# A feed-forward kernel on one core: the first batch's attention in two halves, and layer 1 of the first 512 tokens in two passes

## The chip, the cores and the metric

The kernel runs on one core of a Trainium2 chip. A core has TensorE (matrix products into PSUM, eight banks of 128 x 512 fp32), VectorE (DVE), ScalarE (ACT), GpSimd (POOL) and SyncE (SP), which here only issues DMAs. Each engine works through its own list of instructions in order, and semaphores tie the lists together. The metric is the device time of one execution in microseconds (us).

## What is computed

Eight sequences of 256 tokens with 256 features pass a cross-attention-like block and a feed-forward network of four layers, each with a layer norm in front and a residual behind. Cut to what matters:

```python
def xattn(x, c):                                # x: 8 x 256 x 256, c = ctx: 8 x 120 x 256
    s = einsum('eth,efh->etf', x, c)            # "score"
    h = gelu_tanh(s) * s                        # "gate"
    return einsum('etf,efh->eth', h, c)         # "weigh"

x = x + xattn(layernorm(x), ctx)
t = layernorm(x)
h = silu(t @ w1.T * w1_s) * (t @ w2.T * w2_s)   # layer 1: 256 -> 1024, twice
h = gelu(h @ h1.T * h1_s)                       # 1024 -> 1024
h = gelu(h @ h2.T * h2_s)                       # 1024 -> 1024
x = x + h @ w3.T * w3_s                         # 1024 -> 256
```

## The kernel before

A batch `b` is one sequence, 256 tokens, kept as two halves `j` of 128 tokens (`xs[:, 2b+j, :]`). Two batches make a tile `t` of 512 tokens, which is what the feed-forward layers work on.

**The attention of a batch** is a chain over all engines. DVE takes the statistics of both halves (`stats` = `spread`, two BATCH_NORM_STATS2, and `gather`, two aggregates). POOL makes the reciprocal deviation (`rstd`, two instructions). DVE normalizes (`scale`, one instruction per half). TensorE transposes (`turn(0,b)`). ScalarE copies the result to SBUF (`copy_t`). TensorE multiplies by the context (`score`), ScalarE applies gelu (`act_s`), DVE multiplies (`gate`), TensorE multiplies by the context again (`weigh`), DVE adds the residual (`add_in`). Then comes the second norm in the same way (`stats(1,b)`, `rstd`, `scale(1,b)`, `turn(1,b)`). Its result is split for the fp32r products: ScalarE copies it rounded into `X[..,0,..]` (`first`), and DVE writes what rounding left out into `X[..,1,..]` (`second`, semaphore `s_X1`). Every intermediate of a batch lies in one PSUM bank, `side(b)` = `P[6 + b % 2]`.

**Layer 1 of a tile** is 16 groups `i` of four products (two halves of the contraction, rounded part and rest): `i = 2m` is column block `m` of `w1`, `i = 2m+1` that of `w2`. Six PSUM banks take turns by the table `TURN`. Behind a pair of groups ScalarE does `silu(t,m)` into one of two buffers `SL`, and DVE does `both(t,m)`, which multiplies the second product by it. A group that reuses a bank waits for the `silu` or the `both` that read it (`first_free`, `consumed`). In `layer1(0)` of ScalarE, `hi8` rounds a finished block for the next layer, and DVE's `lo8` takes the rest.

**The order of TensorE around the change** is written out by hand: spins (products whose results nobody reads, `SPIN`), the attention of batches 0 and 1 woven together, then the first six groups of tile 0 for batch 0's 256 columns alone, with `turn(1,1)` behind the fourth. When `s_X1` says that batch 1's columns are there, the same six groups follow for them, and `layer1(0)` does the other ten groups over all 512 columns. `attend` puts `turn(0,2)` and `turn(0,3)` behind group 10. Then `eight(0)` starts on the next layer: eight products, `score(2)` and `score(3)`, and so on. Each of the products `i` of `eight` needs 1 MB of weights, which SP loads back from a DRAM copy into the ring `WR` (`load_w8`), behind other loads in the one queue. The weights of layer 1 are loaded into `stage` and rounded by ScalarE into `W12` (`copy_w(0)` to `copy_w(3)`, semaphore `s_cp`; a group of `w1` needs three of them, one of `w2` all four).

ScalarE needs its Silu table before `silu(0,0)`; the call `table(ACT.Silu)` on a spare tile makes the load stand ahead of it.

## Time and profile before

| | us |
|---|---|
| median of 3 runs | 340.02 |
| lowest and highest | 339.81, 340.51 |
| the profiled execution | 339.02 |
| its span in the profile | 337.1 |

The profile shows one execution. Its busy shares say little here, since TensorE is busy in nearly all of the span; what matters is where TensorE is not, and for whom it waits there. The views to read are the chain of work that ended last, in order of time, and the timelines of the single engines in the first 60 us. In the timelines a row merges instructions of one kind that follow each other; the time in brackets is how long the engine was idle before it, and who ended that. TensorE was granted its full clock in every slice of the page.

### The profile page before, as it was taken

To read this page: it belongs to the slowest core of one execution; us is meant where nothing else is said; L and a number is where in the kernel's file an instruction comes from. 1 tells how busy PE (TensorE), PEld (TensorE's weight loads), DVE (VectorE), ACT (ScalarE), POOL (GpSimd) and SP (SyncE) were. 2 spreads that over 40 slices of the span, in tenths; PEclk is the share of its full clock that TensorE was granted. 3 is DMA by queue.
4 is the path that set the end of the run, shared out by engine and by line. 5 is a ranking of instruction groups with operands and counts; after the bars stand their busy time and mean duration, and the time that the engine had idled before them with its cause. 6 is when DMAs were issued, how large, how long until landed. Compare 5 with 4: busy or idle time off the path is not lost.

```text
span 337.1 us, 4680 instructions
## 1 busy us (share of the span) xinstructions
PE 327.9 (97%) x1628; PEld 276.9 (82%) x1628; DVE 254.0 (75%) x465; ACT 205.0 (61%) x327; POOL 17.9 (5%) x40
## 2 busy tenths in 40 slices
PE   6699999999999999999999999999999999999996
PEld 4588888888888888888899888888888888888895
DVE  4576879639968697897777534697978698977885
ACT  2655625384844464867794244469587769557960
POOL 3130023002202000000000000000000000000000
PEclk9999999999999999999999999999999999999999
DMA  7799999699939769334540550026655636333003
GB/s 231 258 372 408 398 392 405 227 349 383 319 136 325 266 189 328 140 130 144 192 161 0 162 213 0 1 92 243 228 189 187 207 122 234 124 124 126 1 0 134
DMA packets 22541, 68.61 MB, mean 204 GB/s; under 512 B 1632, under 2 KB 3040, under 8 KB 18784
## 3 DMA queue, kind: packets, MB, share of 16 engines
q1 hardware_dynamic: 22512, 68.25, 56.8%
q8 instruction: 15, 0.25, 0.3%
q14 instruction: 14, 0.11, 0.1%
HBM read 57.75 MB, written 18.87 MB: 227 GB/s over the span
## 4 chain that ended last, share of the span: by engine, by line
PE 95%; DVE 2%; DMA 1%; ACT 0%; issue 0%; POOL 0%; SPq 0%; DVEq 0%
PE P L1176 45%; PE P L1240 17%; PE P L1129 17%; PE P L1266 9%; PE P L1077 2%; PE P L1093 2%; PE P L1085 2%; DMA xs<-in_x 1%; DVE st L753 1%; DVE xs L782 0%; DVE X L789 0%; DVE xn L766 0%; SPq L358 0%; POOL rs L472 0%; ACT X L545 0%
## 5 line engine op out<-in xcount | busy, mean ns | idle before, releaser
L1176 PE MATMUL P<-TR,WR 128*128 128x512 f32 x672 | 152.6, 389 | 0.0
L1176 PEld LDWEIGHTS P<-TR,WR 128*128 128x128 f32 x672 | 126.1, 188 | 26.2
L831 DVE TENSOR_TENSOR TR<-H,TR 128x512 fp32r<-128x512 f32 x84 | 57.5, 688 | 19.0 <-ACT TR L569 16.9
L569 ACT ACTIVATE TR<-H 128x512 fp32r<-128x512 f32 x84 | 52.5, 629 | 21.4 <-DVE H L826 16.2
L1129 PE MATMUL P<-X,W 128*128 128x512 f32 (+1 forms) x280 | 60.4, 373 | 2.0 <-DVE X L789 2.0
L1240 PE MATMUL P<-TR,WR 128*128 128x512 f32 x256 | 61.3, 395 | 0.0
L1129 PEld LDWEIGHTS P<-X,W 128*128 128x128 f32 x280 | 49.1, 188 | 11.2 <-DVE X L789 2.4
L1240 PEld LDWEIGHTS P<-TR,WR 128*128 128x128 f32 x256 | 47.8, 188 | 9.7
L804 DVE SCALAR_TENSOR_TENSOR H<-P,sc,SL 128x512 f32<-128x512 f32 x32 | 23.9, 746 | 23.4 <-PE P L1129 18.2
L559 ACT ACTIVATE SL<-P,sc 128x512 f32<-128x512 f32 x32 | 22.1, 690 | 31.7 <-PE P L1129 31.4
L610 ACT ACTIVATE H<-H,sc 128x512 f32<-128x512 f32 x36 | 25.9, 720 | 15.5 <-DVE H L847 15.4
L1266 PE MATMUL P<-WR,TR 128*128 128x256 f32 x256 | 31.3, 283 | 0.0
L826 DVE TENSOR_TENSOR H<-H 128x512 f32<-128x512 f32 x48 | 31.2, 685 | 0.0
L1266 PEld LDWEIGHTS P<-WR,TR 128*128 128x128 f32 x256 | 31.0, 192 | 0.2
L853 DVE SCALAR_TENSOR_TENSOR SL<-SL 128x1024 f32<-128x1024 f32 x22 | 26.8, 1218 | 1.4 <-ACT SL L503 1.4
L847 DVE TENSOR_TENSOR H<-P,H 128x512 f32<-128x512 f32 x36 | 24.4, 684 | 4.0 <-PE P L1176 4.0
L837 DVE TENSOR_TENSOR TR<-H,TR 128x512 fp32r<-128x512 f32 x32 | 20.9, 688 | 6.6 <-ACT TR L590 6.4
L598 ACT ACTIVATE H<-P 128x512 f32<-128x512 f32 x36 | 21.5, 597 | 6.2 <-PE P L1176 3.8
L590 ACT ACTIVATE TR<-H 128x512 fp32r<-128x512 f32 x32 | 19.2, 627 | 2.3 <-PE P L1266 2.3
L503 ACT ACTIVATE SL<-WR 128x1024 f32<-128x1024 f32 x14 | 14.8, 1055 | 9.0 <-DVE SL L853 9.0
L584 ACT ACTIVATE H<-P,sc 128x512 f32<-128x512 f32 x16 | 9.7, 689 | 12.2 <-PE P L1240 12.2
L753 DVE BATCH_NORM_STATS2 st<-xs 128x6 f32<-128x256 f32 x32 | 12.0, 416 | 4.3 <-DMA xs<-in_x 4.0
(50 smaller groups left out, 203.9 us busy)
## 6 DMA issues: line engine op xcount, KB each, us to landing
WR<-blocks_h SPq DMA_DIRECT2D x27, 1024.0 KB, 4.8
H<-in_h SPq DMA_DIRECT2D x8, 1024.0 KB, 12.0
blocks_h<-H SPq DMA_DIRECT2D x8, 1024.0 KB, 6.3
blocks_h<-in_h SPq DMA_DIRECT2D x7, 1024.0 KB, 14.0
stage<-in_w SPq DMA_DIRECT2D x4, 512.0 KB, 7.2
WR<-last_w SPq DMA_DIRECT2D x2, 1024.0 KB, 4.9
xs<-in_x SPq DMA_DIRECT2D x7, 256.0 KB, 11.1
out<-xs SPq DMA_DIRECT2D x6, 256.0 KB, 6.4
```

Of the source, the lines that this page charges most:

```text
L559: eng.activation(SL[:, g % 2, :], P[TURN[t][i % 6]][:, :], ACT.Silu, scale=sc[:, m:m + 1]).then_inc(s_sl, 1)
L569: eng.activation(TR[:, f % RING, 0, :], operand(c, L, s, kk), ACT.Copy).then_inc(s_hi, 1)
L610: eng.activation(to, src, ACT.Gelu, scale=sc[:, col:col + 1]).then_inc(s_ge, 1)
L804: eng.scalar_tensor_tensor(out=source(t // 2, 0)[:, m, t % 2, :], in0=P[TURN[t][i % 6]][:, :], scalar=sc[:, 8 + m:9 + m], in1=SL[:, g % 2, :],
L826: eng.tensor_tensor(tile(src, to, kk), tile(src, one, kk), tile(src, two, kk), ALU.subtract).then_inc(s_td, 1)
L831: eng.tensor_tensor(TR[:, f % RING, 1, :], operand(c, L, s, kk), TR[:, f % RING, 0, :].bitcast(f32), ALU.subtract).then_inc(s_lo, 1)
L847: eng.tensor_tensor(to, bank(c, L, s, m)[:, :], other, ALU.add).then_inc(s_cd, 1)
L853: eng.scalar_tensor_tensor(out=a, in0=a, scalar=1.0, in1=a, op0=ALU.is_ge, op1=ALU.not_equal, accum_out=fl[:, i:i + 1]).then_inc(s_fl, 1)
L1129: out_ = eng.matmul(P[TURN[t][i % 6]][:, lo_:hi_], w, X[:, t % 2, h, k, lo_:hi_], start=(k == 0 and h == 0), stop=(k == 1 and h == 1))
L1176: out_ = eng.matmul(bank(c, L, s, m)[:, :], WR[r % WRING][:, at:at + 128], TR[:, f % RING, h, :], start=(s in FRESH and kk == 0 and h == 0 ...
L1240: out_ = eng.matmul(bank8(i, m)[:, :], WR[r % WRING][:, at:at + 128], TR[:, f % RING, h, :], start=(i % 2 == 0 and kk == 0 and h == 0), st ...
L1266: out_ = eng.matmul(P[n][:, at], TR[:, f % RING, h, j * 128:(j + 1) * 128], WR[r % WRING][:, k * D:(k + 1) * D], start=(k == 0 and h == 0 ...
```

## The change

The attention of batch 0 is done in two halves of 128 tokens, each with its own PSUM bank (`piece(0)` = `P[6]`, `piece(1)` = `P[5]`) and its own semaphores for the first half (`e_...`). For it there are new functions on every engine, one per step, with the same operations on half the elements. Layer 1 of tile 0 becomes two passes of 16 groups over 256 columns, `p = 0` for batch 0 and `p = 1` for batch 1. Both passes have their own `silu` and `both` over 256 columns. `weigh(1)`, `turn(1,1)` and `turn(0,2)` of TensorE are moved into pass one (behind groups 3, 12 and 14), `score(2)` goes between the passes, and `turn(0,3)` stays behind group 10 of pass two. Pass one uses the banks in the order `TURN0`. The spins go to `P[0]`, and the first lot has 16 instead of 20. SP's list of DMAs is unchanged.

On VectorE the first pass stood like this before (from the second norm of batch 1 on):

```order
L766 TENSOR_SCALAR xn<-xs,mv,rs 128x256 x2
L753 BN_STATS st<-xs 128x6 x2
L757 BN_AGGR mv<-st 128x2 x2
L789 TENSOR_TENSOR X<-P,X 128x2x256
L753 BN_STATS st<-xs 128x6 x2
L757 BN_AGGR mv<-st 128x2 x2
L804 SCALAR_TENSOR_TENSOR H<-P,sc,SL 128x512 x2
L766 TENSOR_SCALAR xn<-xs,mv,rs 128x256 x2
L804 SCALAR_TENSOR_TENSOR H<-P,sc,SL 128x512
```

Here L766 is `scale`, L753 and L757 are `stats`, L789 is `second`, L804 is `both`. In the changed kernel (L897 is `both`, L875 `add_in`, L812 and L816 `stats`, L825 `scale`, L882 `second`):

```order
L897 SCALAR_TENSOR_TENSOR H<-P,sc,SL 128x256 x2
L875 TENSOR_TENSOR xs<-P,xs 128x512
L812 BN_STATS st<-xs 128x6 x2
L816 BN_AGGR mv<-st 128x2 x2
L897 SCALAR_TENSOR_TENSOR H<-P,sc,SL 128x256 x2
L812 BN_STATS st<-xs 128x6 x2
L816 BN_AGGR mv<-st 128x2 x2
L897 SCALAR_TENSOR_TENSOR H<-P,sc,SL 128x256
L825 TENSOR_SCALAR xn<-xs,mv,rs 128x256 x2
L897 SCALAR_TENSOR_TENSOR H<-P,sc,SL 128x256
L825 TENSOR_SCALAR xn<-xs,mv,rs 128x256 x2
L897 SCALAR_TENSOR_TENSOR H<-P,sc,SL 128x256 x2
```

Batch 1's residual, its second norm and the statistics of batch 2 have moved from ahead of the first `both` to between the `both` of pass one; right behind these rows stands `second(1)`.

On TensorE pass one ends, and pass two begins, like this in the changed kernel (L1238 is a group, four rows' worth of 128x256 each; L1186 a turn; L1194 `score(2)`; L1348 the first products of `eight(0)`):

```order
L1238 MATMUL P<-X,W 128x256 x8
L1186 MATMUL P<-ident,xn 128x128 x4
L1238 MATMUL P<-X,W 128x256 x4
L1194 MATMUL P<-xt,cf 120x256 x2
L1238 MATMUL P<-X,W 128x256 x44
L1186 MATMUL P<-ident,xn 128x128 x4
L1238 MATMUL P<-X,W 128x256 x20
L1348 MATMUL P<-TR,WR 128x512 x8
L1194 MATMUL P<-xt,cf 120x256 x2
```

Before, 20 wide products stood in front of `eight(0)`, and both scores behind its first eight:

```order
L1129 MATMUL P<-X,W 128x512 x20
L1240 MATMUL P<-TR,WR 128x512 x8
L1085 MATMUL P<-xt,cf 120x256 x4
L1240 MATMUL P<-TR,WR 128x512 x32
L1093 MATMUL P<-ct,hh 128x256 x4
```

On ScalarE the last steps ahead of the first Silu are in another order. Before (L525 is `copy_w`, L545 `first`, L521 the table, L559 `silu`, L577 `hi8`):

```order
L525 ACTIVATE W<-stage 128x1024 x2
L545 ACTIVATE X<-P 128x2x256
L525 ACTIVATE W<-stage 128x1024
L545 ACTIVATE X<-P 128x2x256
L521 ACT_TABLE_LOAD
L521 ACTIVATE spare<-mhalf 128x2
L559 ACTIVATE SL<-P,sc 128x512 x2
```

After (L564 is `copy_w`, L599 the halves of `first`, L570 `copy_t(1)`, L577 `act_s(1)`, L613 `silu`):

```order
L564 ACTIVATE W<-stage 128x1024 x2
L599 ACTIVATE X<-P 128x2x128
L570 ACTIVATE xt<-P 128x512
L564 ACTIVATE W<-stage 128x1024
L599 ACTIVATE X<-P 128x2x128
L564 ACTIVATE W<-stage 128x1024
L577 ACTIVATE gl<-P 120x256
L560 ACT_TABLE_LOAD
L560 ACTIVATE spare<-mhalf 128x2
L613 ACTIVATE SL<-P,sc 128x256 x7
```

`copy_t(1)` and `act_s(1)` of the second batch have moved behind the first batch's halves, and `act_s(1)` now stands right ahead of the table load.

The diff, cut to its core (the halves on DVE, ScalarE and POOL are the old steps over half the elements):

```diff
-SPIN = (20, 3, 3, 4, 4)
+TURN0 = (2, 3, 4, 5, 0, 1)
+SPIN = (16, 3, 3, 4, 4)
...
+        def piece(j):
+            return P[(6, 5)[j]]
...
+        def tokens1(t, p):
+            return slice(p * TB, (p + 1) * TB) if t == 0 else slice(0, TT)
...
@@ ScalarE
             def layer1(t):
+                for m in range(8 if t == 0 else 0):
+                    silu(0, m, 0)
+                    if m == 6:
+                        first(1)
+                    if m == 7:
+                        copy_t(2)
                 for m in range(8):
                     silu(t, m)
                     if t == 0 and m == 6:
-                        copy_t(2)
                         copy_t(3)
...
-            copy_t(0)
-            act_s(0)
+            copy_half(0)
+            act_half(0)
+            copy_half(1)
+            act_half(1)
+            copy_w(0)
+            copy_w(1)
+            first_half(0)
             copy_t(1)
-            copy_w(0)
+            copy_w(2)
+            first_half(1)
+            copy_w(3)
             act_s(1)
-            copy_w(1)
-            copy_w(2)
-            first(0)
-            copy_w(3)
-            first(1)
             table(ACT.Silu)
...
@@ VectorE
             def layer1(t):
+                for m in range(8 if t == 0 else 0):
+                    both(0, m, 0)
+                    if m == 1:
+                        add_in(1)
+                        stats(1, 1)
+                    if m == 3:
+                        stats(0, 2)
+                    if m == 4:
+                        scale(1, 1)
+                    if m == 5:
+                        scale(0, 2)
+                    if m == 7:
+                        second(1)
+                        stats(0, 3)
                 for m in range(8):
                     both(t, m)
-                    if t == 0 and m in (1, 2):
-                        scale(0, m + 1)
+                    if t == 0 and m == 2:
+                        scale(0, 3)
...
+            stats_half(0, 0)
+            stats_half(0, 1)
+            scale_half(0, 0)
+            spread(0, 1)
+            scale_half(0, 1)
+            gather(0, 1)
+            gate_half(0)
+            add_half(0)
+            stats_half(1, 0)
+            gate_half(1)
             scale(0, 1)
+            add_half(1)
+            scale_half(1, 0)
+            stats_half(1, 1)
+            second_half(0)
+            scale_half(1, 1)
+            second_half(1)
             gate(1)
...
@@ TensorE
             def layer1(t):
-                if t:
-                    eng.wait_ge(s_X1, 2 * t + 2)
+                if t == 0:
+                    eng.wait_ge(s_X1, 1)
+                    for i in range(16):
+                        if i < 2:
+                            eng.wait_ge(s_cp, 3 + i)
+                        if i >= 6:
+                            consumed(0, i - 6, 0)
+                        group(0, i, 0).then_inc(s_mm1, 1)
+                        if i == 3:
+                            weigh(1)
+                        if i == 12:
+                            turn(1, 1)
+                        if i == 14:
+                            turn(0, 2)
+                    score(2)
+                eng.wait_ge(s_X1, 2 * t + 2)
                 for i in range(16):
-                    if t == 0 and i < 6:
-                        continue
                     first_free(t, i)
                     group(t, i).then_inc(s_mm1, 1)
                     attend(t, i)
...
             spin(SPIN[0])
-            turn(0, 0)
+            turn_half(0, 0)
             spin(SPIN[1])
-            score(0)
+            score_half(0)
+            turn_half(0, 1)
             spin(SPIN[2])
+            weigh_half(0)
+            score_half(1)
+            spin(SPIN[3])
+            weigh_half(1)
             turn(0, 1)
-            weigh(0)
+            turn_half(1, 0)
+            spin(SPIN[4])
+            turn_half(1, 1)
             score(1)
-            spin(SPIN[3])
-            weigh(1)
-            spin(SPIN[4])
-            turn(1, 0)
-            eng.wait_ge(s_X1, 1)
-            for i in range(6):
-                if i < 2:
-                    eng.wait_ge(s_cp, 3 + i)
-                group(0, i, 0, TB)
-                if i == 3:
-                    turn(1, 1)
-            eng.wait_ge(s_X1, 2)
-            for i in range(6):
-                group(0, i, TB, TT).then_inc(s_mm1, 1)
             layer1(0)
```

## Rows read from the trace of the kernel before

**Rows 1.** The page: DMA share in 40 slices; the chain by engine.
```profile
DMA  7799999699939769334540550026655636333003
...
PE 95%; DVE 2%; DMA 1%; ACT 0%; issue 0%; POOL 0%; SPq 0%; DVEq 0%
```

**Rows 2.** The chain in order of time: start us, length us, what.
```profile
1.63 3.44 DMA xs<-in_x
...
17.01 2.18 PE P L1129 x16
...
20.30 0.70 DVE X L789
...
21.04 7.71 PE P L1129 x44
28.75 0.87 PE P L1077 x8
29.62 4.55 PE P L1129 x20
34.17 1.81 PE P L1240 x8
35.99 1.73 PE P L1085 x8
...
62.15 0.87 PE P L1077 x8
...
172.46 15.35 PE P L1266 x128
```

**Rows 3.** Timeline of TensorE: start us, length us, what, count.
```profile
34.01 1.98 PE L1240 MATMUL P<-TR,WR 128*128 128x512 f32 x8
```

**Rows 4.** Timeline of VectorE, first 26 us.
```profile
3.06 0.79 DVE L753 BATCH_NORM_STATS2 st<-xs 128x6 f32<-128x256 f32 x2 [3.06 <-DMA xs<-in_x]
...
9.57 0.42 DVE L773 TENSOR_TENSOR hh<-P,gl 120x256 f32<-120x256 f32 x1 [1.41 <-ACT gl L538]
11.28 0.69 DVE L782 TENSOR_TENSOR xs<-P,xs 128x512 f32<-128x512 f32 x1 [1.28 <-PE P L1093]
12.01 0.75 DVE L753 BATCH_NORM_STATS2 st<-xs 128x6 f32<-128x256 f32 x2
...
12.96 0.39 DVE L773 TENSOR_TENSOR hh<-P,gl 120x256 f32<-120x256 f32 x1
...
24.89 0.75 DVE L804 SCALAR_TENSOR_TENSOR H<-P,sc,SL 128x512 f32<-128x512 f32 x1
25.55 0.73 DVE L766 TENSOR_SCALAR xn<-xs,mv,rs 128x256 f32<-128x256 f32 x2
```

**Rows 5.** Timeline of ScalarE, first 23 us.
```profile
9.15 0.39 ACT L538 ACTIVATE gl<-P 120x256 f32<-120x256 f32 x1 [1.28 <-PE P L1085]
...
16.01 1.05 ACT L525 ACTIVATE W<-stage 128x1024 fp32r<-128x1024 f32 x1
19.66 0.60 ACT L545 ACTIVATE X<-P 128x512 fp32r<-128x512 f32 x1 [2.61 <-PE P L1077]
20.28 1.28 ACT L521 ACT_TABLE_LOAD   x1
21.58 0.20 ACT L521 ACTIVATE spare<-mhalf 128x2 f32<-128x2 f32 x1
21.89 0.69 ACT L559 ACTIVATE SL<-P,sc 128x512 f32<-128x512 f32 x1
```

**Rows 6.** Timeline of GpSimd, one `rstd` of a batch.
```profile
13.13 0.22 POOL L470 TENSOR_SCALAR rs<-mv 128x2 f32<-128x2 f32 x1 [5.81 <-DVE mv L757]
13.43 0.71 POOL L472 TENSOR_TENSOR rs<-rs,mhalf 128x2 f32<-128x2 f32 x1
```

**Rows 7.** Timeline of SyncE's queue; the 12.95 issue waited for `stage[3]` to land.
```profile
12.95 0.61 SPq L295 DMA_DIRECT2D blocks_h<-in_h  x1
...
44.19 0.42 SPq L308 DMA_DIRECT2D WR<-blocks_h  x1
```

**Rows 8.** DMA issues of 44.15 to 44.45 us, with median us to landing.
```profile
WR<-blocks_h SPq DMA_DIRECT2D x1, 1024.0 KB, 14.4
```

## What the change does to the time: the prediction

> **What bounds the kernel now.** I read the page's chain first: 95% of what ended last is TensorE's work [rows 1], so nothing else can matter for long. The chain in order of time then says where the rest is [rows 2]: up to 17.01 us it hops between all engines through the first batch's attention. From 17.01 TensorE works, loses about half a us before 21.04 (it waits for the second batch's `X`, which DVE starts at 20.30), and from 21.04 on its pieces follow each other without a hole to the end. So only two things can move the time: when the last product of layer 1 of the first 512 tokens is out of TensorE, and how much TensorE work there is. The mark that I compare is the start of the first eight products of `eight(0)`: 34.01 us before [rows 3]. Since the change does `score(2)` ahead of that mark and before did it behind, where two scores took 1.73 us [rows 2], the mark of before that is like for like is 34.01 + 0.87 = 34.88 us.
>
> **TensorE's own cost of two passes.** A product over 256 columns takes 0.120 us (128 in 15.35 us), one over 512 takes 4.55/20 = 0.228 us [rows 2]. Before, 48 narrow and 40 wide ones: 14.9 us. After, 128 narrow ones: 15.4 us. So 0.5 us more work, all of it on the path. A turn is 0.44 us, a score or weigh 0.87 us [rows 2]; these are moved, their number stays. Pass one is 64 x 0.120 + `weigh(1)` 0.87 + two turns 0.87 = 9.4 us; pass two is 7.7 + one turn 0.44 = 8.1 us. The four spins fewer in the first lot are work that nobody waits for: the first transposes wait for the statistics, not for TensorE.
>
> **The prologue in halves.** Sizes I don't have are taken between rows. DVE: 256 elements 0.42 us, 512 0.69 [rows 4]; 128 elements I put at 0.29. ScalarE: 256 at 0.39, a copy of 512 at 0.60 [rows 5], 128 at 0.28. POOL needs 0.31 + 0.71 us for an rstd, plus about 0.1 of hop on either side [rows 6]. Hops between other engines are 0.02 to 0.15 us. The first batch is there when DVE starts at 3.06 [rows 4], the second at 5.07 [rows 2].
> Half 0: statistics to 3.65, rstd to 4.74, scale to 5.25, transposes to 5.75, copy 6.15, score 6.95 (context landed before), gelu 7.25, gate 7.57, weigh 8.38, add 8.82, statistics 9.45, rstd 10.55.
> Half 1 follows through the same engines: its weigh ends at 10.50, its add at 10.94. Then `scale_half(1,0)` to 11.38, statistics of half 1 to 11.89, rstd to 12.99, `scale_half(1,1)` to 13.50, transposes to 14.00, `first_half(1)` to 14.40, `second_half(1)` to 14.85. Group 0 of pass one may start at 14.90, and the next at about 15.45, because ScalarE does `copy_w(3)` (1.05 us [rows 5]) only after `first_half(1)`; its data are there at 12.95 [rows 7]. As group 0 takes 0.48, I count pass one from 14.95 us: 2.06 us earlier than the first products before.
> If that were all, pass two would end at 14.95 + 9.4 + 8.1 = 32.5 and the gain would be 2.4 us. Two new waits eat it.
>
> **New wait one: who feeds pass one.** Behind `first_half(1)` (14.40) ScalarE has `copy_w(3)` to 15.35, `act_s(1)` to 15.64, and then the table load: from 20.28 to the first Silu at 21.89 is 1.61 us [rows 5], so the first Silu starts at 17.27. It lasts 0.48 over 256 columns (0.69 for 512 [rows 5], less 0.21 as between gelu and copy there), so DVE's first product of the pass (`both`) starts at 17.76. A `both` over 256 columns I cost at 0.40 us from start to start: 0.65 for 512 (24.89 to 25.55) less some 0.25 by which 256 elements are cheaper (0.69 to 0.42) [rows 4]. In front of `scale(1,1)` stand five of them, `add_in(1)` (0.72, 11.28 to 12.01) and two rounds of statistics (0.95 each, 12.01 to 12.96 [rows 4]): 2.00 + 0.72 + 1.90 = 4.62. So `scale(1,1)` starts at 22.38 and its second half is out at 23.1. TensorE comes to `turn(1,1)`, which waits for it, at 14.95 + 13 x 0.48 + 0.87 = 22.06 and leaves it at about 23.37 instead of 22.5: 0.9 us lost. Nothing of before shows this wait; there the same turn stood after four groups and only the second batch's own half hung on it. Queued behind it are three groups and `turn(0,2)`: pass one ends at 23.37 + 3 x 0.48 + 0.44 = 25.25.
>
> **New wait two: the hand-over between the passes.** `second(1)` stands behind the last `both` of pass one on DVE. The last product is visible about 0.2 us after TensorE could go on, `both` takes 0.40 to the next start, `second(1)` 0.67, hops 0.08: 1.35 us, of which `score(2)` fills 0.87 without shortening it. Pass two starts at 26.60 and ends at 26.60 + 8.1 = 34.7 us. Within pass two DVE needs for two groups of a column block 0.40 and ScalarE about the same, plus half of a 512-wide split (some 0.3 each): 0.7 against TensorE's 0.96, so no further wait.
>
> **The sum.** 34.7 against 34.88: 0.2 us gained. Behind the mark the order of the work is the same on all engines, and TensorE has no hole there, so the 0.2 us goes to the end. The profiled execution took 339.02 us (span 337.1 and 1.9 around it), it becomes 338.8; the median of the three runs lies 1.0 above it, and I take the difference over to it: 340.02 - 0.2 = 339.8 us.
>
> **A cap further on.** The weights of the fourth product of `eight(0)` are asked for at 44.19 [rows 7] and land 14.4 us later [rows 8], at 58.6. The DMA engines are busy without a break then (the 9s of the page's DMA line from its seventh slice of 8.4 us back to its fourth [rows 1]), so asking earlier doesn't bring them sooner. TensorE comes to them at 62.15 - 1.8 = 60.3 of the chain [rows 2], 60.1 in start times. So no more than about 1.5 us of any gain ahead of them can reach the end: even a perfect pass one stops at 338.5 us. With 0.2 us gained it costs nothing.
>
> **A rule that speaks against the change.** The load of the Silu table lasts 1.28 us, and the small ACTIVATE behind it starts 0.02 us after its end [rows 5]. "ScalarE: Activation LUTs" of the Trainium skill, in What ACT_TABLE_LOAD costs, puts a drain of about 1.38 us beside each load of 1.28 us. This case's rows show no such drain on either side of the load.
>
> **The rivals.**
> A, my forecast: both new waits, 339.8 us; unsure by 0.6 us either way from the prices of the 128-wide steps (each by 0.05, some ten in a row) and of `both`.
> B, DVE is early enough at `turn(1,1)`: should the first Silu start 0.9 us sooner, or the statistics run shorter, only the hand-over is left. Then pass two starts at 14.95 + 9.4 + 1.35 = 25.7 and the mark is at 33.8: 1.1 us gained, 338.9 us. For it: DVE is idle from the end of its prologue to 17.76. Against: the rows of the table load are fixed and ScalarE has `copy_w(3)` and `act_s(1)` in front of it.
> C, the other side: the 256-wide steps of pass one cost nearly as much as 512-wide ones, start to start 0.65 instead of 0.40. Place: the five `both` before `scale(1,1)`, then the last one before `second(1)`. 6 x 0.25 = 1.5 us later, the mark at 36.2: 1.3 us slower, 341.3 us. It is slower than before by what can be measured from a price of 0.55 on. For it: no row of before has this instruction at 256. Against: a TENSOR_TENSOR out of PSUM has 0.42 at 256 [rows 4].
> D, no new wait at all and the cap decides: 338.5 us. It needs `second(1)` ahead of the last `both`, which the order denies.
> E, a drain of 1.4 us in front of or behind the table load that has merely not been visible: both new waits move by it, 34.7 + 1.4 = 36.1, 341.2 us. The rows leave it a chance of 1 in 100. (By the page named above this is what would come.)
>
> **Chances.** A 0.62, B 0.17, C 0.12, D 0.03, E 0.01, something not seen 0.05. What a measurement of this kernel can tell from no change is about 0.2%, or 0.7 us. A reaches beyond that on the fast side in about one case in six, on the slow side in one in fifteen. Faster 0.12 + 0.15 + 0.03 = 0.30; slower 0.04 + 0.12 + 0.01 + 0.02 = 0.19; same 0.51. The range takes in B and most of the way to C: 338.7 to 340.9 us.
>
> **What would show it.** First product of layer 1 at 14.9 (right if 14.6 to 15.4); first Silu at 17.3; a hole or late turn of TensorE of 0.9 us at `turn(1,1)` around 22 to 23.4, released by DVE's `xn`; a second start of layer 1 at 26.6, released by DVE's `X`; `both` over 256 columns at 0.48 us each; `eight(0)` at 34.7; no wait for weights near 60. I am wrong if `both` is above 0.6, if the first Silu is not near 17.3, or if TensorE has holes behind 35 us.

## The result, and the profile after it

| | before, beside it | changed |
|---|---|---|
| median | 339.28 us (22 runs) | 340.43 us (22 runs) |
| lowest and highest | 338.74, 341.57 | 339.99, 341.78 |
| the profiled execution, its span | 339.02, 337.1 | 340.34, 338.6 |

The changed kernel is slower: ratio 1.003, 95% interval 1.0019 to 1.0042. That is 1.0 us, or 1.15 between the medians, where 0.2 us of gain was forecast. In the profiled executions it is 1.3 us, and 1.4 of span (338.56 less 337.13 in the trace's hundredths). 340.43 lies inside the range by luck: of the kernel before, 15 of the 22 executions lie between 338.7 and 339.5 us and seven between 339.8 and 341.6, for a reason that no trace shows, and the three whose median of 340.02 was my base are all among the seven. Counted from 339.28, the forecast would have been 339.1 us and the range 338.0 to 340.2, and 340.43 is outside it.

First the place that I argued about. The timeline of TensorE in the changed kernel, start us, length us, what, and in brackets the idle time ahead and who ended it:

```profile
15.14 2.18 PE L1238 MATMUL P<-X,W 128*128 128x256 f32 x16
17.16 1.03 PE L1202 MATMUL P<-ct,hh 120*128 120x256 f32 x4
17.84 4.67 PE L1238 MATMUL P<-X,W 128*128 128x256 f32 x36
22.87 0.76 PE L1186 MATMUL P<-ident,xn 128*128 128x128 f32 x4 [0.36 <-DVE xn L825]
...
25.80 1.09 PE L1194 MATMUL P<-xt,cf 128*120 128x256 f32 x4 [0.30 <-ACT xt L570]
26.67 5.54 PE L1238 MATMUL P<-X,W 128*128 128x256 f32 x44
...
34.87 2.00 PE L1348 MATMUL P<-TR,WR 128*128 128x512 f32 x8
```

The first products of layer 1 start at 15.14 us instead of 17.01 [rows 2], TensorE then waits at `turn(1,1)` and at the hand-over, and `eight(0)` starts at 34.87 against the like-for-like mark of 34.88. The attention in halves and the passes have cancelled almost exactly.

The piece near 62 us and the last add of VectorE say that nothing happens behind it either. The chain in order of time has

```profile
62.22 0.87 PE P L1186 x8
```

where the kernel before has it at 62.15 [rows 2], and the timeline of VectorE at the end reads, first in the changed kernel, then in the one before:

```profile
334.63 0.42 DVE L1055 TENSOR_TENSOR xs<-Y,xs 128x256 f32<-128x256 f32 x1
```
```profile
334.56 0.42 DVE L962 TENSOR_TENSOR xs<-Y,xs 128x256 f32<-128x256 f32 x1
```

0.07 us later, and yet the span ends 1.4 us later. The rest is behind the last piece of work. VectorE's last step is a branch over the fallback (`with eng.If(v != 0)`, which recomputes everything if a test of the rounding fails and is never entered), and then the DRAIN at the kernel's end. By line (operation, count, durations in ns, first and last start in us), in the changed kernel:

```profile
L1145 DVEq COMPARE_BRANCH  x1: 76/76/76, 335.2 to 335.2; - x1
...
L54 DVEq DRAIN  x1: 61/61/61, 338.3 to 338.3; - x1
...
L54 SPq DRAIN  x1: 7/7/7, 337.2 to 337.2; - x1
```

and in the kernel before:

```profile
L1036 DVEq COMPARE_BRANCH  x1: 76/76/76, 335.1 to 335.1; - x1
...
L52 DVEq DRAIN  x1: 59/59/59, 335.7 to 335.7; - x1
...
L52 SPq DRAIN  x1: 7/7/7, 336.9 to 336.9; - x1
```

The views round to tenths; in the trace's hundredths the exit, from the start of the branch to the start of the DRAIN, took 0.57 us before and takes 3.05 us now. Before, SyncE, which waits until the last output has landed, was the last (336.90); now VectorE is, at 338.27. Not all of the difference is VectorE's: SyncE's own end moved to 337.24, since the last output, issued 0.07 us later, took 1.98 us to land for 1.72. So about 0.3 of the 1.4 us is that landing, and 1.0 us (338.27 less 337.24) is what the exit adds. Neither the page's chain nor a view of waits by work shows this, since no engine is busy; the 95% that the chain gave to TensorE [rows 1] was true, and the difference lies in the part that it leaves out.

### The profile page after: what moved, and what is told of

The parts are those of the page before. It is cut to its first block, busy times and chain, and to the rows that moved or that the text cites. A ratio compares the mean times of both kernels' runs of the same rounds, so it can differ in the third digit from the quotient of the medians.

```text
span 338.6 us, 4807 instructions
## 1 busy us (share of the span) xinstructions
PE 329.3 (97%) x1668; PEld 278.9 (82%) x1668; DVE 256.3 (76%) x476; ACT 207.2 (61%) x338; POOL 19.4 (6%) x44
## 4 chain that ended last, share of the span: by engine, by line
PE 96%; DVE 2%; issue 1%; POOL 0%; ACT 0%; POOLq 0%; DVEq 0%
PE P L1285 45%; PE P L1348 17%; PE P L1238 17%; PE P L1374 9%; PE P L1202 2%; PE P L1186 2%; PE P L1194 2%; PE P L1384 1%; PE P L1437 0%; PE P L1423 0%; DVE xs L851 0%; DVE xn L839 0%; DVE st L832 0%; PE P L1430 0%; ACT xt L570 0%
## 5 line engine op out<-in xcount | busy, mean ns | idle before, releaser
L924 DVE TENSOR_TENSOR TR<-H,TR 128x512 fp32r<-128x512 f32 x84 | 57.5, 689 | 18.5 <-ACT TR L623 16.4
L1238 PE MATMUL P<-X,W 128*128 128x512 f32 (+1 forms) x320 | 61.4, 349 | 0.1
L1348 PE MATMUL P<-TR,WR 128*128 128x512 f32 x256 | 61.4, 395 | 0.0
L1238 PEld LDWEIGHTS P<-X,W 128*128 128x128 f32 x320 | 51.7, 189 | 8.1 <-DVE X L857 0.5
L1348 PEld LDWEIGHTS P<-TR,WR 128*128 128x128 f32 x256 | 47.7, 188 | 9.7
L613 ACT ACTIVATE SL<-P,sc 128x512 f32<-128x512 f32 (+1 forms) x40 | 24.0, 604 | 34.1 <-PE P L1238 33.4
L897 DVE SCALAR_TENSOR_TENSOR H<-P,sc,SL 128x512 f32<-128x512 f32 (+1 forms) x40 | 25.4, 640 | 23.9 <-PE P L1238 16.0
L498 POOL TENSOR_TENSOR rs<-rs,mhalf 128x2 f32<-128x2 f32 x14 | 11.0, 785 | 1.2
```

The lines of the kernel that those rows point to most:

```text
L613: eng.activation(SL[:, g % 2, at], bank1(t, 2 * m, p)[:, at], ACT.Silu, scale=sc[:, m:m + 1]).then_inc(s_sl, 1)
L897: eng.scalar_tensor_tensor(out=source(t // 2, 0)[:, m, t % 2, at], in0=bank1(t, 2 * m + 1, p)[:, at], scalar=sc[:, 8 + m:9 + m], in1=SL[:, ...
L924: eng.tensor_tensor(TR[:, f % RING, 1, :], operand(c, L, s, kk), TR[:, f % RING, 0, :].bitcast(f32), ALU.subtract).then_inc(s_lo, 1)
L1238: out_ = eng.matmul(bank1(t, i, p)[:, at], w, X[:, t % 2, h, k, at], start=(k == 0 and h == 0), stop=(k == 1 and h == 1))
L1348: out_ = eng.matmul(bank8(i, m)[:, :], WR[r % WRING][:, at:at + 128], TR[:, f % RING, h, :], start=(i % 2 == 0 and kk == 0 and h == 0), st ...
```

## The experiments

**The fallback shorter.** In the changed kernel the fallback's loops ran over 7 batches instead of 8 on every engine, so the branch skips 194, 27 fewer.

```diff
-                for b in range(NB):
+                for b in range(NB - 1):
```

> The changed kernel, with the fallback at the end (the branch that is never taken in these runs) written for 7 batches instead of 8 on every engine; the eighth batch of the fallback is left out, nothing of what is executed is. On VectorE the jump over the fallback gets 25 instructions shorter. Theory 1 (the lost time is VectorE's jump over the fallback: 3.0 us from the branch to the next instruction in the changed kernel, 0.5 us before, because the place it jumps to has to be fetched): VectorE leaves its last block near 335.8 instead of 338.3, span 337.1 to 337.3, time 1.3 us less than the changed kernel, so 0.0 to 0.1% above the kernel before. Theory 2 (the end takes longer because the kernel has 11 semaphores more or because the 256-column passes cost later): nothing changes, ratio to before 1.003, span 338.6.

Measured: 339.14 us, ratio 0.9982 [0.9961, 1.0004]. The exit is short again, from 335.4 us to

```profile
L54 DVEq DRAIN  x1: 59/59/59, 336.0 to 336.0; - x1
```

So the whole loss goes away with code that is never run. Its semaphores and its order of work are the changed kernel's: that rival falls.

**The kernel before, 11 instructions longer.** Eleven one-column memsets on VectorE while it waits for the first data:

```diff
+            for i in range(11):
+                eng.memset(padt[:, i:i + 1], 0.0)
```

> The kernel before, with 11 writes of one column of a spare tile at the start of VectorE's list, where it has 3 us of idle time, so that VectorE executes as many instructions ahead of its last branch as in the changed kernel. Theory 1 (the place of VectorE's branch in its list of instructions decides whether the place it jumps to is at hand): VectorE leaves its last block 2.5 us later, span 338.5, time 1.3 to 1.5 us above before (ratio 1.004), with TensorE's last product where it was. Theory 2 (semaphores, or the attention halves themselves): no change, ratio 1.000.

Measured: 340.32 us, ratio 1.0028 [1.001, 1.0046], and the same long exit:

```profile
L1039 DVEq COMPARE_BRANCH  x1: 76/76/76, 335.3 to 335.3; - x1
...
L52 DVEq DRAIN  x1: 64/64/64, 338.2 to 338.2; - x1
```

Eleven tiny instructions at the start of the kernel before cost as much as the whole change. This is the cleanest evidence, since nothing of the change is in it. The number 11 was meant to bring the branch to the changed kernel's place, which is really 21 further on; that 11 is slow as well was luck.

**The changed kernel with 117 and with 107 instructions more.** With 107, 27 stand at the start and 5 behind each of 16 late `both` (shown here); with 117, 5 at the start and 7 behind each. With 107 the list is 128 longer than before, with 117 it is 138.

```diff
+            for i in range(27):
+                eng.memset(padt[:, i:i + 1], 0.0)
...
+                    for i in range(5 if t >= 2 else 0):
+                        n = 27 + 40 * (t - 2) + 5 * m + i
+                        eng.memset(padt[:, n:n + 1], 0.0)
```

> The changed kernel with 117 writes of one column of a spare tile on VectorE, 5 at its start and 7 behind each of the 16 last multiplications of layer 1, where it waits for TensorE. Before the change VectorE ran 11 instructions less, so its branch now stands 128 instructions behind the place it had before the change; the instruction fetches in the trace are 8192 bytes, which would be 128 instructions of 64 bytes. Theory 1 (the place within such a block decides): VectorE's jump is short again, 0.5 us, span 337.1 to 337.4 and ratio 1.000 to 1.001, although the list is longer than ever. Theory 1b (more instructions make it longer whatever their place): the jump stays at 3 us, ratio 1.003. Theory 2: as 1b, span 338.6.

> The changed kernel with 107 writes of one column of a spare tile on VectorE (27 at its start, 5 behind each of the 16 last multiplications of layer 1). Counted in the traces, waits that are instructions of their own included, VectorE's list has 631 records in the changed kernel and 610 before the change, 21 more and not 11; with 117 more it stood 10 past a full block of 128, where the jump was still long, as with 11 more ahead of the kernel before. With 107 it stands exactly 128 behind the kernel before. Theory 1 (place within a block of 8192 bytes): the time from VectorE's branch to its next instruction falls from 3.0 to 0.5 us, span 337.2, ratio to before 1.000 plus what the 107 writes cost VectorE, at most 0.3 us. Theory 1b (the longer the list, the worse): 3.0 us, ratio 1.003.

Measured: 117 gives 340.45 us, ratio 1.003 [1.0015, 1.0044], exit 3.04 us. The number 117 came from the page's count of VectorE's busy instructions, which grew by 11 (465 to 476); the list itself grew by 21, so this run stands at 138, ten past a full 128, and is long like the kernel before with its 11 more. 107 gives 339.12 us, ratio 0.9999 [0.9984, 1.0015], exit 0.58 us:

```profile
L1151 DVEq COMPARE_BRANCH  x1: 76/76/76, 334.9 to 334.9; - x1
...
L54 DVEq DRAIN  x1: 60/60/60, 335.5 to 335.5; - x1
```

The kernel of the change, complete, with 107 useless instructions more, is as fast as the one before. "The longer the slower" falls, and a period of 128 fits.

**Which places are slow.** The kernel before with 64 and with 107 memsets more, one execution each:

> The kernel before with VectorE's list 64 one-column memsets longer (32 at its start, 2 behind each of 16 late `both`), so about 674 records instead of 610. The jump over the fallback skips some 220 instructions. Theory (it is slow when two borders of a block of 128 instructions lie between the branch and its target, quick when only one does; the borders follow from the runs so far: the target of the kernel before is less than 11 instructions ahead of one): 64 further on the branch is still in the same block and the target in the one behind the next, so the exit takes 3 us and the span grows by 1.2 to 1.5 us. Rival (only a target in the first few dozen places behind a border is slow): the target is some 55 places behind the border, the exit takes 0.6 us, the span 337.1 to 337.4.

> The kernel before with VectorE's list 107 one-column memsets longer (27 at its start, 5 behind each of 16 late `both`), so about 717 records. Theory (number of borders between branch and target): 107 further on the branch has passed the next border itself, only one lies between it and the target again, the exit takes 0.6 us and the span stays at 337.1 to 337.4. Rival (short only where the target stands at the end of a block, as in the kernel before and 128 later): the target is 96 to 107 places behind the border, not at the end, the exit takes 3 us, the span 338.4 to 338.8.

Measured: 64 gives 340.41 us, span 338.6; 107 gives 338.97 us, span 337.2; the kernel before ran 339.46 beside them. The exits, of 64 first, then of 107:

```profile
L52 DVEq DRAIN  x1: 61/61/61, 338.3 to 338.3; - x1
```
```profile
L52 DVEq DRAIN  x1: 59/59/59, 335.8 to 335.8; - x1
```

The traces so far together, with the place counted from the kernel before:

| kernel | branch, places on | skipped | exit us | span us |
|---|---|---|---|---|
| before | 0 | 221 | 0.57 | 337.1 |
| before, 11 more | 11 | 221 | 2.87 | 338.4 |
| changed | 21 | 221 | 3.05 | 338.6 |
| before, 64 more | 64 | 221 | 3.06 | 338.6 |
| before, 107 more | 107 | 221 | 0.58 | 337.2 |
| changed, 107 more | 128 | 221 | 0.58 | 337.2 |
| changed, 117 more | 138 | 221 | 3.04 | 338.9 |
| changed, short fallback | 21 | 194 | 0.57 | 337.4 |

The span of the row of 64 says little: its last output took 2.75 us to land (1.70 to 2.04 in the other traces), so that SyncE ended at 338.14 us and the exit added only 0.2 us. What it shows is the exit of 3.06 us.

One rule holds for all eight rows, and for the six traces of the experiments further down (places 5, 16 and three times 21 with 194 skipped, and 128 with 221, all short): with borders every 128 instructions, the exit is short where one border lies between branch and target, long where two do. The target of the kernel before lies less than 11 places ahead of a border; 11, 21 and 64 further on it is behind it, at 107 the branch itself has crossed the border below, and with 27 instructions fewer to skip the target falls back ahead of it. The exits of 64 and 107 came out as written down beforehand. The rows don't prove the counting of borders, though: that an exit is long wherever the target stands in the first 60 or so places of a block, and short from about 100 on, fits them too, wherever the branch is. What they do show is that the target's place matters (with 221 and 194 skipped the branch is at the same place 21), and that both 0 and 128 are short while 11 and 138 are long. The mechanism behind it, that the target's block must first be fetched, the traces bear out only in part: instruction packets of one queue average 8 KB,

```profile
q14 instruction: 14, 0.11, 0.1%
```

and from VectorE's branch to the end of the trace there are two such packets in each of the four traces with a long exit, and one in each of the ten others. But which packet VectorE waited for I could not tell. In "Runtime: NRT & Kernel Launch" of the Trainium skill, under Instruction fetch mechanics, it says that a taken branch with a target outside the current two pages of instructions has to wait for a fetch. The direction agrees with the 3.05 us. The size of 256 instructions that the same section gives for a page of instructions doesn't: a jump over 221 would then never leave two neighbouring ones, and the rows fit a period of 128.

**The halves alone.** The first batch's attention in halves, but layer 1 as before (six groups over 256 columns, then wide ones), with `weigh(1)` behind the fourth group and `turn(1,1)` behind the sixth; the fallback short, as in all that follow but the last.

```diff
-            turn(0, 0)
+            turn_half(0, 0)
...
             eng.wait_ge(s_X1, 1)
             for i in range(6):
...
                 group(0, i, 0, TB)
```

> The kernel before with the first part of the change alone (attention of batch 0 in halves, the order of that part as in the changed kernel), layer 1 of the first 512 tokens as before, turn(1,1) behind the first six half groups; fallback for 7 batches. Theory A (the halves make batch 0 early at batch 1's cost, which only two passes can use): the first product of layer 1 at 15.1, TensorE then idle from about 19 until batch 1's columns are there at 22.7, eight(0) at 35.5 instead of 34.0, ratio 1.0045. Rival (the halves are a gain of their own): eight(0) at or before 34.0.

Measured: 344.01 us (4 runs), ratio 1.0167 [1.0108, 1.0225]. TensorE:

```profile
14.92 2.18 PE L1213 MATMUL P<-X,W 128*128 128x256 f32 x16
...
21.46 0.88 PE L1161 MATMUL P<-ident,xn 128*128 128x128 f32 x4 [2.53 <-DVE xn L808]
23.75 9.93 PE L1213 MATMUL P<-X,W 128*128 128x256 f32 x44 [1.41 <-DVE X L865]
...
38.94 1.98 PE L1324 MATMUL P<-TR,WR 128*128 128x512 f32 x8
```

The page's clock line, and ScalarE's first Silu:

```profile
PEclk9978999999999999999999999999999999999999
```
```profile
25.08 0.69 ACT L600 ACTIVATE SL<-P,sc 128x512 f32<-128x512 f32 x1 [0.59 <-PE P L1213]
```

The direction was right, the size far off: 38.94 us where I had written 35.5. The second start of layer 1 is at 23.75 us where I had written 22.7, and the 44 products behind it take 9.93 us for 7.71 [rows 2]. The latter is TensorE's clock: it was idle from 18.9 to 21.46 us and again, but for four transposes, to 23.75, and from 22.0 to 28.6 us the granted clock was 0.50, the lower of its two levels (1.2 GHz), and full again from 28.8 us on, after TensorE had worked without a hole since 23.75. Before 28.8 us a product over 256 columns takes 0.21 us from start to start for 0.12; from there on a product over 512 takes 0.23, as before. No bank is missing: TensorE waits for nothing after 23.75, and the first Silu waits 0.59 us for TensorE. In the changed kernel the clock stays full. Without the passes the early first products are of no use: TensorE runs out of work for batch 0, waits for batch 1, and loses 2.2 us more to the clock.

**The passes alone.** The attention whole, layer 1 in two passes; `turn(1,1)` behind group 3, `second(1)` behind the second `both`.

```diff
+                for m in range(8 if t == 0 else 0):
+                    both(0, m, 0)
+                    if m == 1:
+                        second(1)
```

> The two passes alone: the first batch's attention stays whole as before (first products of layer 1 near 17.0 us), layer 1 of the first 512 tokens in two passes of 256; `turn(1,1)` stays behind group 3 and `second(1)` stands behind the second `both` of pass one, so that nothing hangs on the hand-over. The fallback that the branch jumps over is cut to 7 batches, so that VectorE's exit is short. Theory (the halves bring the first product 2 us forward, the two waits and the half us of narrow products eat it; each part has its own share): first Silu 18.7 instead of 21.9, pass one 17.0 + 64 x 0.120 + two turns 0.87 = 25.6 us, no hole between the passes, pass two 8.1 and `score(2)` 0.87: `eight(0)` at 34.6 us, 0.3 us ahead of the like-for-like 34.88 of before; ratio 0.999. Rival (two passes cost more than the count of products says, because ScalarE or VectorE can't keep up with 256-wide groups while they also do `first(1)` and `second(1)`): holes of TensorE within pass one, `eight(0)` behind 35.5, ratio 1.002 or more.

Measured: 339.33 us, ratio 1.0014 [0.9997, 1.0031]: not to be told from before.

```profile
16.89 2.17 PE L1223 MATMUL P<-X,W 128*128 128x256 f32 x16 [1.54 <-DVE X L876]
...
25.99 1.09 PE L1179 MATMUL P<-xt,cf 128*120 128x256 f32 x4 [0.30 <-ACT xt L565]
...
35.03 2.00 PE L1333 MATMUL P<-TR,WR 128*128 128x512 f32 x8
```

35.03 us against 34.6 expected: pass one runs without a hole, though in 8.8 us for the 8.55 counted, and `score(2)` then waits 0.30 us for ScalarE's copy of the third batch, a wait I hadn't reckoned with here. No engine failed to keep up, so the rival for this run falls. With the halves the mark was 34.87: coming 1.75 us earlier at the start (15.14 against 16.89), they have brought 0.16 us at the mark.

**Feeding pass one better.** If the two waits eat the gain, taking away what makes them should return it. First the statistics of the third batch ahead of the first `both`, and the scales earlier (GpSimd's order to match):

```diff
             gate(1)
+            stats(0, 2)
...
-                    if m == 3:
-                        stats(0, 2)
-                    if m == 4:
-                        scale(1, 1)
-                    if m == 5:
-                        scale(0, 2)
+                    if m == 2:
+                        scale(0, 2)
+                    if m == 3:
+                        scale(1, 1)
```

> The changed kernel with the fallback for 7 batches (its eighth batch left out, nothing that is executed), and on VectorE the statistics of batch 2 moved from behind the fourth multiplication of pass one to the idle time ahead of the first, scale(0,2) behind the third and scale(1,1) behind the fourth; GpSimd takes batch 2's deviation ahead of batch 1's second. Theory A (VectorE's lateness at turn(1,1) costs TensorE what the prediction said): turn(1,1) leaves TensorE 0.7 us sooner, pass two starts at 25.9 instead of 26.7, eight(0) at 34.1 instead of 34.9, and as VectorE's jump is short too, 0.7 us below the kernel before, ratio 0.998. Rival (pass one is bound by TensorE and the hand-over alone, or gives the time back at the weights near 60 us): eight(0) at 34.7 to 34.9 or a wait for weights behind it, ratio 1.000.

Then, besides, `second(1)` ahead of the last `both`, and `score(2)` behind group 2 of pass two:

```diff
-                    if m == 7:
+                    if m == 6:
                         second(1)
+                    if m == 7:
                         stats(0, 3)
...
-                    score(2)
                 eng.wait_ge(s_X1, 2 * t + 2)
...
+                if (t, i) == (0, 2):
+                    score(2)
```

> As the kernel with batch 2's statistics moved, and the hand-over between the passes taken away: second(1) stands ahead of the last multiplication of pass one, and score(2) behind the third group of pass two instead of between the passes. Theory A: TensorE goes from pass one into pass two without a hole, pass two starts at 24.8, eight(0) at 33.8, ratio 0.997; the wait for the weights of the fourth product of eight(0) (59 to 60 us) is still not reached. Rival (the DMA cap is nearer than 1.5 us): TensorE waits there and the ratio stays at 0.998 or above.

Measured: the first 338.70 us, ratio 0.9989 [0.9972, 1.0006], `eight(0)` at 34.22 us; the second 338.29 us, ratio 0.9964 [0.9947, 0.998], `eight(0)` at 33.68. Both marks came within 0.12 us of what was expected. In the second, pass two follows pass one without a hole:

```profile
22.21 0.67 PE L1186 MATMUL P<-ident,xn 128*128 128x128 f32 x4
...
24.04 2.29 PE L1238 MATMUL P<-X,W 128*128 128x256 f32 x16
26.16 1.03 PE L1194 MATMUL P<-xt,cf 128*120 128x256 f32 x4
26.83 4.18 PE L1238 MATMUL P<-X,W 128*128 128x256 f32 x32
...
33.68 2.00 PE L1348 MATMUL P<-TR,WR 128*128 128x512 f32 x8
```

So the two waits cost 1.2 us at the mark (34.87 less 33.68) of the 1.87 us by which the first products come earlier. The rest is work that the change puts between the first products and the mark: `weigh(1)`, 0.87 us, stood ahead of them before, and the narrow products take 0.5 us more; against that, the wait of 0.47 us ahead of 21.04 is gone. This adds up to within about 0.2 us. And the cap further on shows, although I had expected that it would still not be reached. The chain of the second version, in order of time:

```profile
45.37 14.64 DMA WR<-blocks_h
60.01 0.04 issue
60.05 2.11 PE P L1348 x8
```

TensorE waits 0.8 us there for the weights of the fourth product, and the profiled execution, the slowest of its ten, gives the gain back (339.07 us); the median doesn't.

**The loads of batches 6 and 7 behind those weights.** 0.5 MB ahead of them less, once with the short fallback, once with the whole one and the 107 memsets:

```diff
-            load_x(6)
-            load_x(7)
             load_raw(3)
             sums_out(0)
             load_w8(3)
+            load_x(6)
+            load_x(7)
```

> The version with the feeding of pass one reordered (statistics of the third batch ahead of the first `both`, `second(1)` ahead of the last one, `score(2)` in pass two; fallback of 7 batches) and, besides, the loads of batches 6 and 7 (0.5 MB) put behind the load of the fourth product's weights in SyncE's list. Theory (the cap: those weights land at a time set by how many bytes stand ahead of them, at 370 to 400 GB/s, not by when they are asked for): they land 0.5 MB / 0.39 = 1.3 us earlier, near 58.6 us instead of 60.0; the wait of 0.8 us for `WR` near 60 is gone, the last add of VectorE comes 0.8 us earlier than without the move, ratio 0.9945 to 0.996. Rival (the wait is set by the round trip of the stored block or by the queue's order of service): landing stays near 60, the wait of 0.3 to 0.8 us stays, ratio 0.9965 as without the move.

> The same order and the same moved loads with the whole fallback, as the changed kernel has it, and VectorE's list 107 one-column memsets longer (27 at its start, 5 behind each of 16 late `both`), which puts the jump over the fallback at the same place in a block of 128 instructions as in the kernel before. Theory (the place decides): VectorE's exit takes 0.6 us, 738 or so of its instructions in the trace; the gain ahead reaches the end but for some 0.1 to 0.3 us that the memsets cost: ratio 0.995 to 0.997, faster than both kernels. Rival (the place that is good for one list is not good for another one, the code around the loops moved too): exit of 3 us, ratio 1.001 to 1.003.

Measured: 338.19 us, ratio 0.9968 [0.9954, 0.9982], and 338.28 us, ratio 0.997 [0.9955, 0.9984]. In both traces the wait is gone, the exit is short, and the last add of VectorE starts about 1 us earlier than before (the second version):

```profile
33.82 1.55 PE L1354 MATMUL P<-TR,WR 128*128 128x512 f32 x6
```
```profile
333.60 0.42 DVE L1058 TENSOR_TENSOR xs<-Y,xs 128x256 f32<-128x256 f32 x1
```

The ratio, however, is no better than without the moved loads, and the landing (57.5 and 58.4 us) isn't clearly earlier than elsewhere: 58.4 in the passes alone, run beside them with the loads in their old place, and 58.6 to 60.0 in the other traces. What the move itself brings stays open; it is not shown. The version with 107 memsets has the changed kernel's complete work and is faster than both kernels: 338.28 us against 339.12 beside it.

## Why the prediction was wrong, and where it was right

**The step that failed** is in the sum: "Behind the mark the order of the work is the same on all engines, and TensorE has no hole there, so the 0.2 us goes to the end", and with it the tail that I carried over unchanged from the profiled execution. The order behind the mark is the same and TensorE has no hole; still 0.2 us of gain became 1.0 us of loss, because the end isn't TensorE's. VectorE's way out over the skipped fallback went from 0.57 to 3.05 us, and what of it exceeds SyncE's end, 1.0 us in this trace, was added. The prediction puts down nothing for the 21 instructions by which VectorE's list grows, nor for the branch behind them. The case "something not seen" had a chance of 0.05; this was it. No rival of mine had the right mechanism. The runs show this part twice over: taking it away (the short fallback, 107 memsets more) makes the change even, adding it to the kernel before (11 memsets, and in one execution 64) costs the same 1 us. The base of 340.02 was a second fault, 0.74 us above the median of 22 executions; it made the time look better forecast than it was.

**TensorE's own cost, and the prologue.** First products at 15.14 us for 14.95; 0.19 us late, within what sizes taken between rows allow. Pass two took 8.20 us for the 8.12 counted. One side sum was wrong: "the gain would be 2.4 us" without the waits compares an end without `score(2)` with a mark that has it; like for like it is 34.88 less 33.3, or about 1.5 us. The new waits were thus forecast to cost 1.4 us, and the reordered version measures them at 1.2. The sum of 34.7 isn't touched, as its 1.35 us has `score(2)` in it. In the chances, one case in six of A's 0.62 is 0.10, not 0.12.

**Wait one.** Its end is right to a tenth: the timeline of VectorE shows the chain that I summed.

```profile
17.88 0.88 DVE L897 SCALAR_TENSOR_TENSOR H<-P,sc,SL 128x256 f32<-128x256 f32 x2 [1.57 <-ACT SL L613]
18.67 0.68 DVE L875 TENSOR_TENSOR xs<-P,xs 128x512 f32<-128x512 f32 x1
...
22.04 0.45 DVE L897 SCALAR_TENSOR_TENSOR H<-P,sc,SL 128x256 f32<-128x256 f32 x1
22.41 0.73 DVE L825 TENSOR_SCALAR xn<-xs,mv,rs 128x256 f32<-128x256 f32 x2
```

First `both` at 17.88 (17.76 forecast), `scale(1,1)` at 22.41 (22.38), five `both`, `add_in(1)` and two rounds of statistics in 4.53 us (4.62). The group behind the turn starts at 23.39 (23.37). As TensorE came to the turn 0.2 us late, the wait took 0.7 us where I had 0.9. A `both` over 256 columns goes at 0.40 from start to start (0.88 for two in a row, 0.48 each): case C, with 0.65, is out, and so is case B, in which VectorE is early enough. The experiment in which it was made early put the mark 0.65 us ahead of the changed kernel's.

**Wait two.** Pass two starts at 26.67 us for 26.60. But there are two reasons that end together: `second(1)` is out at 26.61, and `score(2)`, which I had put under it for free, only begins at 25.80 because it waits 0.30 us for ScalarE's copy of the third batch. I had named only the first. The mark came at 34.87 for 34.7: pass two started 0.07 us late and took 0.08 more than counted. The late first product is no part of this, since it vanished in wait one.

**The Silu table.** The load stands as before: 1.28 us, the small ACTIVATE behind it 0.01 us later, the first Silu at 17.28 for 17.27. That it hits to a hundredth is luck: the load starts at 15.87, 0.2 us later than I had it, and from there to the first Silu are 1.41 us, not the 1.61 carried over.

```profile
15.87 1.28 ACT L560 ACT_TABLE_LOAD   x1
17.16 0.20 ACT L560 ACTIVATE spare<-mhalf 128x2 f32<-128x2 f32 x1
17.28 0.82 ACT L613 ACTIVATE SL<-P,sc 128x256 f32<-128x256 f32 x2
```

So case E is out, and the drain of 1.38 us that "ScalarE: Activation LUTs" of the Trainium skill puts beside the load is not seen here.

**The cap.** Right in kind: with the mark at 33.68 and 34.22 us TensorE waits 0.8 and 0.3 us for the fourth product's weights, which land near 60 us. The landing follows the issue only loosely: with the loads in their old place, weights asked for between 44.2 and 46.3 us land between 58.4 and 60.0, the later ones rather later, but those of the halves alone, asked for at 48.1, at 59.2. I had put the cap at "no more than about 1.5 us"; it varies by more than 1 us between executions.

## What to carry to other kernels

Compare the ends of all engines, not only the chain of work: a change of a few instructions on one engine can move a branch over skipped code across a border and cost more than the change was meant to bring, so try the same kernel with a few dozen, and with some hundred, empty instructions more before judging an edit worth 1 us. An earlier start of the engine that bounds is worth only what its feeders can follow with; sum up the feeder's queue in front of each instruction that it will wait for, as 1.2 of 1.9 us went there. And where that sum names the instruction in the way, move it: with the exit short, three edits of the order (statistics earlier, `second(1)` one place ahead, `score(2)` later) took the mark 1.2 us ahead and the median from 339.14 to 338.29 us, a gain of 0.4% on the kernel before beside it. And before a slow stretch of TensorE is laid on banks or buffers, look at the clock that it was granted.

## What the runs showed of the hardware that I had not expected

The taken branch over VectorE's fallback took 0.57 to 0.59 us in ten traces and 2.87 to 3.06 us in four, by the place of its target in a grid of 128 instructions; nothing in between was seen. Of the 2.3 to 2.5 us more, 0.9 to 1.2 showed in the times. ScalarE's jump over its fallback takes 2.6 to 3.0 us in every trace, also with the short fallback; in the kernel before it goes from 330.8 us to the DRAIN at 333.5:

```profile
L52 ACTq DRAIN  x1: 81/81/81, 333.5 to 333.5; - x1
```

It costs nothing there, since ScalarE is done early; whether the same rule holds for it wasn't tried. TensorE's granted clock was 0.50 (1.2 GHz) for 6.6 us after it had been idle for 2.5 us in the halves alone, and 2.2 us were lost by it. And a DMA queue that is full can loosen the landing from the issue: over all runs the load of the fourth product's weights was issued between 44.2 and 48.1 us and landed between 57.5 and 60.0.
